# Order of ScalarE's work in a linear-attention and expert kernel: squares of q before den's logarithm, statistics split, exponentials in pairs

## The chip, the cores and the metric

The kernel runs on one NeuronCore of a Trainium2 chip, as one program. The metric is the time of one execution on the device in microseconds; the median of three runs counts, and one more execution was taken with the hardware profiler. In the rows below PE is TensorE, PEld its weight loads, DVE is VectorE, ACT is ScalarE, POOL is GpSimd and SP is SyncE, whose queue (SPq) issues most of the transfers.

## The reference, cut to what matters

x has 16 batches of 512 tokens of width 128. The layer is an adaptive layer norm block: attention with random features, then a feed-forward part in which each token goes to one of eight experts.

```python
mod = (silu(c) @ wmod).reshape(16, 6, 1, 128)      # sa, ca, ga, sb, cb, gb; ga and gb kept away from 0
h = layernorm(x) * (1 + ca) + sa
q, k = feature(h @ Wq.T + bq), feature(h @ Wk.T + bk)     # 16 heads of 8, 32 features each
#   feature(u) = (exp(u @ orf.T / 8**0.25 - sum(u*u) / (2 * sqrt(8))) + 1e-6) / sqrt(32)
kv, ksum = k^T v, sum_l k
attn = (q kv) / (q ksum)
x = x + ga * (attn @ Wo.T + bo)
h = layernorm(x) * (1 + cb) + sb
e = argmax(h @ gate_W + gate_b)
x = x + gb * (gelu(h @ W1[e] + b1[e]) @ W2[e] + b2[e])
```

All of it is computed in fp32.

## The kernel before, in words

Each engine has a program of its own, written out by hand; the order on an engine is the order in the code, and semaphores tie the engines together. There is no planner. The first stage runs `over_batches`: for each of the 16 batches every engine's `batch(b, ...)` runs once. Work on three neighbouring batches is interleaved: the features and attention of batch b, the projections of b+1, the residual and second norm of b-1, the gate and ranks of b-2.

PE's order in a batch (L1261 to L1294) is: `k_features` (L1145, L1148), `transpose_h2` (L1222), `v_project` (L1130), `out_project` of b-1 (L1214), `gate` (L1229), `q_features` (L1165), the gate transpose, `transpose_xn` of b+1 (L1115), `kv_product` (L1181), `project` k of b+1 (L1123), `rank`, `kv_transpose` (L1190), `project` q of b+1, `attend` (L1198, L1202 den, L1205 numerator).

ScalarE's order (L625 to L654): four exponentials of k (L609), v values, four exponentials of q (L615) with `modulate` of b+1 (L571, makes hT) in their middle, `kvm_copy` (L590), for b+1 `k_values` (L578), `k_squares` (L582) and `q_values` (L596), then Ln of den (L648), Exp of its negative (L650, a first value of 1/den in rden), `q_squares` of b+1 (L600), and half of the first norm of b+2 (L565).

VectorE's `attention` takes rden, refines it in two steps (L820, L823) and writes oT (L827), which `out_project` waits for. Ahead of it stand the masked kv (L806), the ranks, eps (L816) and the second norm's scaling of h2 (L725, L736); behind it, at the head of the next `batch`, `x_stats` (L702, four bn_stats, for b+3), the other half of the first norm (L774), the residual (L835) and its statistics (L842). The statistics feed GpSimd's `rstd1_of`, which raises to the power -0.5 (L466).

q's features need the values of q and their squares side by side in one row group. SP's `mix_q` copies them there: two transfers of qvals (L363), issued when q_values is done, then two of qsqs (L366) when q_squares is done, both into qmix, which `q_features` waits for. In the same queue stand the fetches of x, of the modulation rows and of the expert weights.

At the start, PE multiplies the modulation: columns for the first norm (L1103, L1104), then rows in two products (L1107 into bank KV, L1108 into bank G), and VectorE makes the modulation rows of them (L780 to L797); after that come the statistics of batch 1 and `normalise1` of batch 1 (L774).

The second stage has NBLK = 71 blocks of 128 tokens, each of one expert. For block k PE does `hidden` (L1319), the transpose of block k+1 (L1312) and `second` of k-2 (L1332); ScalarE Gelu (L682); VectorE three steps of `result` (L1044 to L1049); GpSimd the indirect store (L535). The block table for the first EARLY = 45 blocks is made before the last batches are routed, the rest later. SP fetches the blocks twelve ahead (`load_block`, L424), and among its fetches writes a padding row block behind each of the eight expert lists (L436); the blocks from 45 on are fetched only when the paddings have landed.

Of the kernel before, what the change touches and what calls it, by code (L numbers as in the profile page):

```python
# [21 lines left out]
F32 = mybir.dt.float32  # L22
# [10 lines left out]
P = 128  # L33
# [12 lines left out]
EARLY = (KNOWN * L - E * (P - 1) + P - 1) // P  # L46
PITCH = NT * P + P
# [32 lines left out]
R_END = R_NORMQ + P  # L80
# [33 lines left out]
def build(nc, x, weights, consts, rows, wmod, firsts, w2, out):  # L114
# [3 lines left out]
    with ExitStack() as ctx:  # L118
# [5 lines left out]

        def sem(name):
            return ctx.enter_context(nc.semaphore(name))
# [10 lines left out]
        feat_q = sb("feat_q", [P, 2, P // 2])  # L137
        bv_cols = sb("bv_cols", [P, D])
# [29 lines left out]
        kf = sb("kf", [P, LT, NC, 2, HP + 1])  # L168
# [41 lines left out]
        kf_row = kf[:, :, :, :, :].rearrange("p t c j k -> p (t c j k)")  # L210
# [3 lines left out]
        F = [pb("ps_feat0"), pb("ps_feat1")]  # L214
        KV, G = pb("ps_kv"), pb("ps_den")
        H, I = pb("ps_out"), pb("ps_gate")
        PJ = [pb("ps_proj0"), pb("ps_proj1")]
# [3 lines left out]
        QB = [F[0], F[1], PJ[0], PJ[1]]  # L221
        Q_ORDER = (2, 3, 0, 1)
        QB0 = [F[0], F[1], G, I]
        counts = [H[:, 0:E], I[:, 2 * P + LT * E:2 * P + LT * E + E]]
# [110 lines left out]
        def _(sp):  # L335
# [57 lines left out]
            mix_q(0)  # L393
# [35 lines left out]
            for k in range(EARLY - E):  # L429
                load_block(k)  # L430

            sp.wait_ge(s_cnti, 1)
            for e in range(E):
                load_block(EARLY - E + e)
                count = sp.value_load(cnt_i[0:1, e:e + 1], min_val=0, max_val=NT * P)
                sp.dma_start(lists[bass.ds(count + e * PITCH, P), :], padding[:]).then_inc(s_pad, 16)  # L436
            for v in range(B - HOMES, B):
                sp.wait_ge(s_scat[v % HOMES], scattered(v))
# [113 lines left out]
        def _(act):  # L552
# [54 lines left out]
            def k_feature(b, c):  # L607
                act.wait_ge(s_feat, 2 * NC * b.v + c + 1)
                a.activation(kf[:, :, c, :, 0:HP], QB[c][:, :].rearrange("p (t j m) -> p t j m", t=LT, j=2), ACT.Exp)\  # L609
                    .then_inc(s_exp, 1)  # L610

            def q_feature(b, n, first=False):
                act.wait_ge(s_feat, 2 * NC * b.v + NC + n + 1)
                c = Q_ORDER[n]
                a.activation(qf[:, c, :], (QB0 if first else QB)[c][:, :], ACT.Exp).then_inc(s_exp, 1)  # L615

# [8 lines left out]
            def batch(b, first=False, second=False, last=False, ahead=True):  # L625
                k_feature(b, 0)
                if not first and not second:
                    h2T_copy(b + -2)
                k_feature(b, 1)
                k_feature(b, 2)  # L630
                k_feature(b, 3)
# [3 lines left out]
                q_feature(b, 0, first)  # L635
                q_feature(b, 1, first)
                if not last:
                    modulate(b + 1)
                q_feature(b, 2, first)
                q_feature(b, 3, first)  # L640
                kvm_copy(b)
                if not last:
                    k_values(b + 1)
                    k_squares(b + 1)
                    q_values(b + 1)
                act.wait_ge(s_den, b.v + 1)
# [4 lines left out]
                if not last:  # L651
                    q_squares(b + 1)
# [43 lines left out]
        def _(dve):  # L696
            v = nc.vector

            def x_stats(b, slot):

                for t in range(LT):
# [58 lines left out]
            dve.wait_ge(s_modc, 1)  # L760

            v.tensor_copy(sa[:], F[0][:, 0:B])
            v.tensor_scalar(ca1[:], F[0][:, B:2 * B], 1.0, None, ALU.add).then_inc(s_cols, 1)

# [13 lines left out]
            normalise1(Batch(0), lo=LT // 2)  # L778
            dve.wait_ge(s_modp, 1)
# [193 lines left out]
            def batch(b, first=False, second=False, last=False, ahead=True):  # L973
# [4 lines left out]
                if ahead:  # L978
# [3 lines left out]
                    dve.wait_ge(s_x[(b + 3).par], 16 * (b + 3).half + 16)  # L982
                    if b.par == 0:
                        first_moments(b.half + 2, marked=x_stats(b + 3, 1))
                    else:
                        x_stats(b + 3, 0)
# [28 lines left out]
                if last:  # L1015
                    for k in range(1, R4 - 1):
                        copy_firsts(k)
                attention(b)
                if last:
# [13 lines left out]
                                   op0=ALU.mult, op1=ALU.add).then_inc(s_fq, 1)  # L1033
# [420 lines left out]
```

## Time and profile before

| | us |
|---|---|
| median of 3 runs | 364.83 (364.52 to 366.34) |
| the profiled execution | 363.67 |
| its span in the trace | 361.9 |
| PE busy in the span | 340.8 (94%) |
| DVE, ACT, POOL busy | 269.2, 270.1, 214.1 |

The page gives busy time by engine, a strip of 40 slices, the transfers, the chain of work that ended last, and the costliest groups of instructions. A timeline row gives the start, the length, the engine, the source line, the operation, what it writes and reads, how many instructions the row merges, and in brackets how long the engine had been idle before it and what released it. Matmuls are pipelined: a row's length reaches into the next row. An average over the span says little here, since the attention batches (to about 211 us) and the expert blocks have different limits; so the rows below are of single stretches.

### The profile page before, as it was taken

How to read it: one execution, taken by the hardware profiler on the slowest of the kernel's cores; microseconds unless marked ns; L12 is line 12 of the kernel's file. 1: busy time of each engine (PE TensorE's matmuls, PEld its weight loads, DVE VectorE, ACT ScalarE, POOL GpSimd, SP SyncE). 2: the span in 40 equal slices, each digit the busy share in tenths (PEclk: the TensorE clock that was granted, in tenths of full speed). 3: DMA queues.
4: the chain of work that ended last, by engine and by line, in shares of the span. 5: the costliest groups of instructions: out<-in, count | busy, mean ns of one | idle time of the engine just before them, and what ended most of it. 6: DMA issues, size and time to landing. Idle time of an engine off the chain costs nothing.

```text
span 361.9 us, 13820 instructions
## 1 busy us (share of the span) xinstructions
PE 340.8 (94%) x4835; PEld 265.8 (73%) x4835; DVE 269.2 (74%) x1103; ACT 270.1 (75%) x708; POOL 214.1 (59%) x262
## 2 busy tenths in 40 slices
PE   7799998899999999999999899999999998999993
PEld 6546664665566566646665679999999997999993
DVE  3706887988898889878887978787777764666653
ACT  2668997898899888988998766666666665666761
POOL 3223285785786767857864618855767554445554
PEclk9989999999999999999999999999999999999999
DMA  6275456866665656434442466544655664645400
GB/s 220 79 247 205 132 192 217 270 217 203 193 240 166 199 192 229 163 129 160 154 144 87 165 170 210 153 139 128 188 177 179 201 213 135 194 122 152 126 37 12
DMA packets 40532, 60.94 MB, mean 168 GB/s; under 512 B 5490, under 2 KB 28278, under 8 KB 40336
## 3 DMA queue, kind: packets, MB, share of 16 engines
q1 hardware_dynamic: 34096, 43.00, 39.6%
q0 software_dynamic: 6368, 17.05, 12.4%
q8 instruction: 41, 0.67, 0.8%
q14 instruction: 27, 0.22, 0.2%
HBM read 28.56 MB, written 19.34 MB: 132 GB/s over the span
## 4 chain that ended last, share of the span: by engine, by line
PE 51%; ACT 17%; DMA 12%; issue 6%; SPq 6%; DVE 3%; POOL 3%; DVEq 0%; POOLq 0%; ACTq 0%
PE ps_proj L1332 12%; DMA qmix<-qsqs 8%; PE ps_feat L1319 7%; PE ps_proj L1123 6%; ACT qf L615 4%; PE ps_proj L1165 4%; PE ps_den L1319 3%; PE ps_kv L1319 3%; ACT shared L571 3%; ACT shared L578 2%; ACT qvals L596 2%; POOL out L535 2%; ACT den L648 2%; PE ps_out L1312 2%; PE ps_kv L1214 2%
## 5 line engine op out<-in xcount | busy, mean ns | idle before, releaser
L535 POOL DMA_INDIRECT out<-kf,modb x71 | 70.5, 993 | 53.4 <-DVE kf L1049 46.5
L497 POOL DMA_INDIRECT experts_lists<-pay,slot x64 | 66.1, 1034 | 42.2 <-DVE slot L883 28.1
L1332 PE MATMUL ps_proj<-w2sb,qf 128*128 x568 | 74.8, 275 | 0.0
L1332 PEld LDWEIGHTS ps_proj<-w2sb,qf 128*128 128x128 f32 x568 | 68.9, 192 | 0.1
L673 ACT ACTIVATE xT<-ps_out 128x128 f32<-128x128 f32 x71 | 19.7, 277 | 46.2 <-PE ps_out L1312 46.1
L1044 DVE TENSOR_TENSOR kf<-ps_proj,firsts_sb 128x128 f32<-128x128 f32 x71 | 20.6, 290 | 36.9 <-PE ps_proj L1332 26.3
L682 ACT ACTIVATE qf<-ps_feat,shared 128x128 f32<-128x128 f32 x144 | 40.9, 374 | 0.0
L1319 PE MATMUL ps_feat<-xT,shared 128*128 128x128 f32 x288 | 38.7, 277 | 1.2 <-issue 0.7
L1319 PEld LDWEIGHTS ps_feat<-xT,shared 128*128 128x128 f32 x288 | 35.0, 192 | 2.4 <-issue 1.7
L1123 PE MATMUL ps_proj<-shared,wsb 128*128 128x512 f32 x62 | 33.3, 620 | 1.3 <-ACT shared L571 0.4
L967 DVE COPY shared<-firsts_sb 128x516 f32 x71 | 30.7, 433 | 1.3 <-issue 1.2
L1145 PEld LDWEIGHTS ps_feat<-feat_w,shared 32*128 32x128 f32 x256 | 19.4, 186 | 13.1 <-ACT shared L582 13.1
L1145 PE MATMUL ps_feat<-feat_w,shared 32*128 32x128 f32 x256 | 26.5, 283 | 0.5 <-ACT shared L582 0.5
L1145 PE MATMUL ps_proj<-feat_w,shared 32*128 32x128 f32 x256 | 26.5, 283 | 0.0
L1148 PE MATMUL ps_feat<-csb,shared 32*128 32x128 f32 x256 | 24.9, 270 | 0.0
L1148 PE MATMUL ps_proj<-csb,shared 32*128 32x128 f32 x256 | 24.9, 270 | 0.0
L615 ACT ACTIVATE qf<-ps_proj 128x512 f32<-128x512 f32 x30 | 16.3, 595 | 10.6 <-PE ps_feat L1165 10.6
L1047 DVE TENSOR_TENSOR kf<-kf,modb 128x128 f32<-128x128 f32 x71 | 21.3, 300 | 2.4
L1049 DVE TENSOR_TENSOR kf<-kf,modb 128x128 f32<-128x128 f32 x71 | 20.9, 294 | 2.4
L1165 PE MATMUL ps_proj<-qmix,feat_q 32*64 32x512 f32 x120 | 16.3, 611 | 5.7 <-DMA qmix<-qsqs 5.1
L491 POOL TENSOR_TENSOR xall<-xall,bog 128x512 f32<-128x512 f32 x16 | 20.5, 1281 | 1.3
L1312 PE MATMUL ps_out<-csb,modb 128*128 128x128 f32 x71 | 19.4, 274 | 1.8 <-DMA modb<-experts_lists 1.7
(189 smaller groups left out, 898.8 us busy)
## 6 DMA issues: line engine op xcount, KB each, us to landing
modb<-experts_lists SPq DMA_DIRECT2D x71, 196.0 KB, 2.6
xall<-in_x SPq DMA_DIRECT2D x16, 256.0 KB, 3.0
qmix<-qvals SPq DMA_DIRECT2D x32, 128.0 KB
qmix<-qsqs SPq DMA_DIRECT2D x32, 128.0 KB
pay<-modb SPq DMA_DIRECT2D x16, 256.0 KB, 2.8
modb<-modulation_rows SPq DMA_DIRECT2D x4, 768.0 KB, 5.1
firsts_sb<-in_firsts SPq DMA_DIRECT2D x8, 322.0 KB
w2sb<-in_w SPq DMA_DIRECT2D x8, 256.0 KB
```

Source lines behind the costliest of these rows:

```text
L497: g_.indirect_dma_start(out=lists, in_=pay[b.home][:, t, :], in_offset=None, out_offset=bass.IndirectOffsetOnAxis(ap=slot[b.home][:, t:t + ...
L535: g_.indirect_dma_start(out=rows_out, in_=yb[u], in_offset=None, out_offset=bass.IndirectOffsetOnAxis(ap=token, axis=0), bounds_check=last ...
L615: a.activation(qf[:, c, :], (QB0 if first else QB)[c][:, :], ACT.Exp).then_inc(s_exp, 1)
L682: ins = a.activation(g[k % R4][:, c * P:(c + 1) * P], HID[k % R4][:, c * P:(c + 1) * P], ACT.Gelu, bias=firsts_c[k % R4][:, WB1 + c:WB1 + ...
L967: v.tensor_copy(firsts_c[k % R4], firsts_sb[:, bass.ds(expert[k] * WB, WB2)]).then_inc(s_fc, 1)
L1123: mm((bank or PJ[i])[:, :], wsb[:, i * P:(i + 1) * P], hT[:], start=True, stop=True).then_inc(s_proj, 1)
L1145: mm(QB[c][:, tokens], kvals[at, tokens], feat_w[at, :], start=True, stop=False)
L1148: ins = mm(QB[c][:, tokens], ksqs[at, tokens], norm_w[at, :], start=False, stop=True)
L1165: ins = mm(bank[c][n * HP:(n + 1) * HP, :], feat_q[at, n, :], qmix[at, n, :], start=True, stop=True)
L1312: tr(XT[:, 0:P], xin[k % U][:, H2:H2 + D], ident).then_inc(s_bt, 1)
L1319: ins = mm(HID[u % R4][:, c * P:(c + 1) * P], firsts_c[u % R4][:, c * P:(c + 1) * P], xT[u % 2][:], start=True, stop=True)
L1332: ins = mm(Y[u % 2][:, 0:D], g[u % R4][:, c * P:(c + 1) * P], w2sb[:, bass.ds(e * DFF + c * D, D)], start=(c == 0), stop=(c == FC - 1))
```

## The change

In the batches, q_squares(b+1) moves on ScalarE ahead of Ln and Exp of den(b). VectorE takes the statistics of the first two tiles of batch b+4 ahead of `attention(b)`, and only those of the last two tiles at their old place. The eight exponentials of a batch become four, each over two neighbouring PSUM banks; for that the feature tile kf is laid out by channel first, and the banks are allocated in pairs. The waits on their count are rewritten.

At the start, batch 0 makes q's features without qmix: a second weight tile feat_v multiplies qvals and a third multiplies qsqs, into the same banks, and SP's `mix_q(0)` goes. The two products of the modulation rows stand behind the transposes of batch 0 and behind its two projections, in place of 12 fill-in matmuls; the copies of the modulation columns stand behind the half of the first norm.

In the block stage the paddings are written beside the fetches of blocks 33 to 40 in place of 37 to 44, and in the last turn `second(68)` stands ahead of `hidden(70)`.

```diff
+PADS_FROM = EARLY - E - 4
...
-            mix_q(0)
...
-            for k in range(EARLY - E):
+            for k in range(PADS_FROM):
                 load_block(k)
             sp.wait_ge(s_cnti, 1)
             for e in range(E):
-                load_block(EARLY - E + e)
+                load_block(PADS_FROM + e)
                 count = sp.value_load(cnt_i[0:1, e:e + 1], min_val=0, max_val=NT * P)
                 sp.dma_start(lists[bass.ds(count + e * PITCH, P), :], padding[:]).then_inc(s_pad, 16)
+            for k in range(PADS_FROM + E, EARLY):
+                load_block(k)
...
+            def k_pair(b, n):
+
+                act.wait_ge(s_feat, 2 * NC * b.v + 2 * n + 2)
+                a.activation(kf[:, 2 * n:2 * n + 2, :, :, :].rearrange("p c t j k -> p (c t j) k")[:, :, 0:HP],
+                             QP[n][:, :, :].rearrange("p c (g m) -> p (c g) m", m=HP), ACT.Exp).then_inc(s_exp, 1)
+
+            def q_pair(b, n, first=False):
+
+                act.wait_ge(s_feat, 2 * NC * b.v + NC + 2 * n + 2)
+                c = Q_ORDER[2 * n]
+                a.activation(qf[:, c:c + 2, :], (QP0 if first else QP)[c // 2][:, :, :], ACT.Exp).then_inc(s_exp, 1)
...
                     q_values(b + 1)
+                    q_squares(b + 1)
                 act.wait_ge(s_den, b.v + 1)
                 act.wait_ge(s_eps, b.v + 1)
                 a.activation(den[:], G[:], ACT.Ln, bias=kveps[:, 1:2]).then_inc(s_denp, 1)
                 act.wait_ge(s_denp, b.v + 1)
                 a.activation(rden[:], den[:], ACT.Exp, scale=-1.0).then_inc(s_rden, 1)
-                if not last:
-                    q_squares(b + 1)
...
             normalise1(Batch(0), lo=LT // 2)
+            mod_columns()
             dve.wait_ge(s_modp, 1)
...
+                    tiles = range(LT) if first else range(LT // 2, LT)
                     if b.par == 0:
-                        first_moments(b.half + 2, marked=x_stats(b + 3, 1))
+                        first_moments(b.half + 2, marked=x_stats(b + 3, 1, tiles))
                     else:
-                        x_stats(b + 3, 0)
+                        x_stats(b + 3, 0, tiles)
...
+                if b.v + 4 < B:
+                    dve.wait_ge(s_x[(b + 4).par], 16 * (b + 4).half + 16)
+                    x_stats(b + 4, b.par, range(LT // 2))
                 attention(b)
...
+            v.tensor_scalar(feat_v[:], rsb[:, R_ORFQ:R_ORFQ + P], float(DH ** -0.25), None, ALU.mult).then_inc(s_fq, 1)
...
-            mm(KV[0:B, 0:3 * D], sc, wmod_sb[:, 0:3 * D], start=True, stop=True)
-            mm(G[0:B, 0:3 * D], sc, wmod_sb[:, 3 * D:6 * D], start=True, stop=True).then_inc(s_modp, 1)
...
+                if first:
+                    for c in Q_ORDER:
+                        at = slice(c * CW, (c + 1) * CW)
+                        mm(QB0[c][:, :], feat_v[at, :], qvals[at, :], start=True, stop=False)
+                    for c in Q_ORDER:
+                        at = slice(c * CW, (c + 1) * CW)
+                        mm(QB0[c][:, :], rsb[at, R_NORMV:R_NORMV + P], qsqs[at, :], start=False, stop=True).then_inc(s_feat, 1)
+                    return
...
             transpose_xn(start)
-            keep_busy(12)
+            mm(KV[0:B, 0:3 * D], sc, wmod_sb[:, 0:3 * D], start=True, stop=True)
             project(start, 0, first=True)
             project(start, 1, first=True, bank=I)
+            mm(G[0:B, 0:3 * D], sc, wmod_sb[:, 3 * D:6 * D], start=True, stop=True).then_inc(s_modp, 1)
...
+                if k == NBLK - 1:
+                    second(k - 2, e)
                 hidden(k)
```

## Rows read from the trace of the kernel before

**Rows 1.** The page's first line, the whole span.
```profile
span 361.9 us, 13820 instructions
```
**Rows 2.** Busy time by windows of one batch each: PE, PEld, DVE, ACT, POOL, clock, DMA.
```profile
47.60:60.60 13.00, 11.85 (x221) 7.43 (x220) 10.53 (x44) 10.90 (x22) 9.73 (x12) 1.00 0.63 210
85.79:97.80 12.01, 11.85 (x220) 7.43 (x220) 10.92 (x53) 10.90 (x22) 8.01 (x11) 1.00 0.65 207
```
**Rows 3.** Timeline of ScalarE in batch 6 and at the head of the next.
```profile
99.57 0.69 ACT L596 ACTIVATE qvals<-ps_proj,wsb 128x512 f32<-128x512 f32 x1
100.14 0.69 ACT L648 ACTIVATE den<-ps_den,kveps 128x512 f32<-128x512 f32 x1
100.86 0.63 ACT L650 ACTIVATE rden<-den 128x512 f32<-128x512 f32 x1
101.40 0.61 ACT L600 ACTIVATE qsqs<-qvals 128x512 f32<-128x512 f32 x1
...
106.61 1.09 ACT L615 ACTIVATE qf<-ps_proj 128x512 f32<-128x512 f32 x2 [0.41 <-PE ps_feat L1165]
```
**Rows 4.** Timeline of VectorE in the same batch.
```profile
100.19 1.14 DVE L736 SCALAR_TENSOR_TENSOR pay<-pay,rstd,modb 128x128 f32<-128x128 f32 x4
101.53 0.76 DVE L820 SCALAR_TENSOR_TENSOR ps_den<-ps_den,kveps,rden 128x512 f32<-128x512 f32 x1 [0.20 <-ACT rden L650]
...
103.05 0.75 DVE L827 SCALAR_TENSOR_TENSOR oT<-ps_kv,kveps,rden 128x512 f32<-128x512 f32 x1
```
**Rows 5.** Timeline of PE in the same batch.
```profile
97.47 0.31 PE L1190 MATMUL ps_den<-csb,kvT 128*128 128x128 f32 x1
...
103.94 1.07 PE L1214 MATMUL ps_kv<-wo,oT 128*128 128x128 f32 x8
...
107.23 1.11 PE L1181 MATMUL ps_kv<-kf,v 128*32 128x65 f32 x64
...
109.51 0.31 PE L1190 MATMUL ps_den<-csb,kvT 128*128 128x128 f32 x1
```
**Rows 6.** Timeline of SP's queue in the same batch, the copies into qmix.
```profile
100.28 1.12 SPq L363 DMA_DIRECT2D qmix<-qvals  x2
102.04 1.11 SPq L366 DMA_DIRECT2D qmix<-qsqs  x2
```
**Rows 7.** Timeline of PE: the output projections of batches 0, 1 and 14.
```profile
30.42 1.16 PE L1214 MATMUL ps_kv<-wo,oT 128*128 128x128 f32 x8
...
35.40 0.27 PE L1190 MATMUL ps_den<-csb,kvT 128*128 128x128 f32 x1
...
41.83 1.07 PE L1214 MATMUL ps_kv<-wo,oT 128*128 128x128 f32 x8
...
202.06 1.06 PE L1214 MATMUL ps_kv<-wo,oT 128*128 128x128 f32 x8
```
**Rows 8.** Timeline at the start, and one window with its clock (columns of rows 2).
```profile
9.13 0.66 PE L1115 MATMUL ps_out<-csb,shared 128*128 128x128 f32 x4
9.24 0.28 DVE L780 COPY modrow<-ps_den 16x128 f32<-16x128 f32 x1 [0.81 <-PE ps_den L1108]
...
14.85 1.12 DVE L774 TENSOR_SCALAR shared<-xall,rstd,shift 128x128 f32<-128x128 f32 x4 [1.83 <-POOL shift L468]
...
18.88 0.65 PE L1165 MATMUL ps_den<-qmix,feat_q 32*64 32x512 f32 x2 [2.52 <-DMA qmix<-qsqs]
...
21.39 1.80 PE L1181 MATMUL ps_kv<-kf,v 128*32 128x65 f32 x64
...
19.00:21.00 2.00, 2.00 (x19) 0.78 (x20) 0.00 (x0) 0.64 (x2) 0.00 (x0) 0.62 0.94 356
```
**Rows 9.** Timeline of PE around the first block of the late table.
```profile
303.60 0.33 PE L1312 MATMUL ps_out<-csb,modb 128*128 128x128 f32 x1 [1.73 <-DMA modb<-experts_lists]
303.80 1.15 PE L1332 MATMUL ps_proj<-w2sb,qf 128*128 x8
```
**Rows 10.** Timeline of GpSimd, the last store.
```profile
358.30 0.97 POOL L535 DMA_INDIRECT out<-kf,modb  x1 [0.30 <-issue]
```

## What the change will do: the prediction

> **What bounds the kernel now.** The program has two stages: sixteen batches of attention (to about 211 us of a span of 361.9 us [rows 1]) and then 71 expert blocks. I read the trace in three steps: busy time by windows, to see which engine fills a batch; then the timelines of the four engines over one batch, laid side by side; then the two ends of the program by themselves.
>
> Two windows of one batch each [rows 2] hold the same work. The one from 85.79 us lasts 12.01 us with PE busy 11.85; the one from 47.60 us lasts 13.00 with the same 11.85. So a batch costs 12.0 us when PE is full, and up to 1 us more when it isn't. From the output projection of batch 1 (41.83) to that of batch 14 (202.06) [rows 7] there are 13 periods in 160.23 us, a mean of 12.325: 4.2 us above 13 x 12.0. The chain of waits puts that excess on the landing of q's squares in qmix, for which L1165 waits.
>
> The reader should not stop there, since a second chain runs beside PE. In batch 6: the kv transpose L1190 starts at 97.47 [rows 5]; behind it ScalarE goes without a pause through kvm, k, q values (99.57), Ln of den (100.14), its Exp (100.86) and q's squares (101.40) [rows 3]; VectorE's reciprocal step L820 starts at 101.53, having waited for rden, and oT (L827) ends at 103.05 + 0.75 = 103.80 [rows 4]; the output projection L1214 starts at 103.94 [rows 5]. An idle PE would start it 0.04 behind oT (other rows of such a hand-over: Exp ends 101.49, L820 starts 101.53), so this chain has 0.14 - 0.04 = 0.1 us to give and no more. I measured L1190's start to oT's end at 6.33 here.
>
> **The change, part by part.** *q's squares ahead of Ln.* q_squares waits for q_values' end: 99.57 + 0.69 + 0.03 = 100.29. It is 0.61 long, and instructions in a row overlap by about 0.1 (99.57 + 0.69 = 100.26, yet Ln starts at 100.14), so it adds 0.52 and Ln starts at 100.81 in place of 100.14 [rows 3]: 0.67 later, and Exp, the three VectorE steps and oT with it. What it gives: SP issues the two qvals transfers from 100.28 for 1.12 us, so the first of qsqs cannot be issued at 100.91, when the data is there, but at 101.42, against 102.04 before [rows 6]: only 0.62 earlier. L1165 then asks 0.6 later and the data lands 0.62 earlier, 1.2 in all, which is more than the longest excess of a batch (1.0 [rows 2]). So every wait for qmix goes, and what is late next is oT. New cycle, from L1190's start: 6.33 + 0.67 + 0.04 = 7.04 to L1214's start; 5.57 from there to the next L1190 at 109.51 [rows 5], of which 0.05 was the wait for qmix, so 5.52; and 0.09 because L1214 now starts from an idle PE (1.16 long at 30.42, 1.07 at 103.94 [rows 7, 5]). Sum 12.65 a batch; over 13 periods 164.45 against 160.23: **+4.2 us**. Bounds: if the 0.1 of give is 0.2, 12.55 and +2.9; if a transfer is still late now and then, 12.75 and +5.5. I take 12.65, since batch after batch L1214 starts 0.12 to 0.14 behind oT as here.
>
> *Half of the statistics ahead of the reciprocal.* It moves two of four bn_stats (0.86 for four, so 0.43) in front of L820. VectorE's h2 scaling ends at 101.33 [rows 4], so the two end near 101.8, and rden now comes at 102.16: hidden, with 0.3 to spare (0.1 to 0.25 where GpSimd stretches L736 to 1.45). Behind oT the residual comes 0.4 earlier, but it was already waiting for L1214: nothing. Its new wait is for an x that was fetched over a batch before. Queued behind that wait are the reciprocal and all that hangs on it. Cost 0, bounds 0 and +0.3 a batch.
>
> *Paired exponentials.* Two single ones take 1.09, and ScalarE was idle 0.41 before them, waiting for PE [rows 3]. All four row groups of L1165 end together, so waiting for two banks costs nothing, and saving 0.07 to 0.2 a pair shortens idle time. Behind the first pair modulation meets the end of L1181 within 0.05, so PE gains nothing either. Cost 0, bounds -0.1 and +0.1 a batch. The Trainium skill (ScalarE: Activation LUTs, "What ACT_TABLE_LOAD costs") has back-to-back ACTIVATEs overlap by about 93 ns of a fixed 186; by an estimate from it a pair would save 0.09, inside the bounds above.
>
> *First chain.* q_features(0) loses its transfer: PE waited 2.52 us for it until 18.88 [rows 8]. What is late next is another: the transposes of batch 1 need normalise1(1), which stood at 14.85. The row products of the modulation (end about 9.2) are moved: the G half behind both projections. hT comes 0.9 earlier (the transposes, at 9.13 [rows 8], stood behind L1107 and L1108, while their input was there at 8.3), the projections, a ScalarE step later, run from 9.8 to 11.8, the G product to 12.5. VectorE's block that began at 9.24 now begins at 12.5, 3.25 later, and normalise1(1), which follows statistics and GpSimd's power step in a fixed row, moves from 14.85 to 18.1 and ends at 19.2; the transposes run from 19.3 in place of 20.3. feat_v adds 0.2 on VectorE and is ready at 16.5, q's features end near 17.9. Then L1181, 1.80 at the low clock (granted 0.62 in the window from 19 us, [rows 8]) and 1.11 at the full one [rows 5]. With the clock low as before the shift of L1190 is -1.1, at the full clock -2.1; I take the middle, -1.6. The extra 0.67 on the way to oT leaves -0.9 for L1214(0), at 29.5 in place of 30.42 [rows 7]. The period after it: 4.98 to L1190(1) (30.42 to 35.40 [rows 7]), 7.04 to L1214: 41.5 in place of 41.83: **-0.3 us**. Bounds -1.0 (full clock, no cold start) and +0.7 (nothing gained).
>
> *Padding.* SP's loop of eight loads and paddings starts four blocks earlier. Before, the load behind the last padding came late: PE stood 1.73 us until 303.60, and with the refill (the first products from an idle PE take 0.33 and 1.15) it cost 2.0 to 2.25 [rows 9]. The loads 33 to 36 that are pushed back wait for stores anyway, and each has 10 us until its use; the load in question moves about 9 us forward. **-2.2 us**, bounds -2.3 and -1.7.
>
> *Last results.* second(68) runs ahead of hidden(70). GpSimd's last stores follow each other at its own pace, 0.97 and 0.30 between, the last at 358.30 [rows 10]. Now result 68 is ready 0.9 earlier (eight products: L1214's 1.07 [rows 5] less the overlap), but hidden(70) and its Gelu come 0.9 later and the last product waits for that: store 70 at about 357.8. **-0.5 us**, bounds 0 and -0.8.
>
> **Sum.** Between batch 14 and block 0 VectorE's table work hangs on oT and shifts as it does. 363.67 (the profiled execution) + 4.2 - 0.3 - 2.2 - 0.5 = 364.9, so +1.2 us. The profiled execution lies 1.16 below the median of the three runs, 364.83; on the median that is **366.0**.
>
> **Rivals.** (1) *The chain through den has more give than I read.* Matmul ends in a trace are modelled; if oT may come 0.67 later without holding PE, only the waits for qmix go and the batch falls to 12.0: 13 x 12.0 = 156 in place of 160.2, with the start about 1 us better: 364.83 - 4.2 - 1.0 - 2.7 = 356.9. For it: PE was the full engine and its waits were for the DMA. Against: 0.1 us of give in all batches. Chance 0.10. The Trainium skill (DMA: Bandwidth & Descriptors, "Rules for kernel authors") says to issue a DMA early and wait on it late; by that rule alone this rival is the forecast. Half-way, at 12.35 a batch (PE regains some of it in hand-overs that I took as fixed), gives 366.0 - 3.9 = 362.1. Chance 0.12. (2) *The statistics hold the reciprocal up.* It decides where L736 ends later than rden minus 0.43, about 101.75 in the batch shown. Half of the batches have GpSimd beside L736; with 0.2 to 0.4 more in each of 14, +2.8 to +5.6: 368.8 to 371.6. Against: L736 ends at 101.33 and the new rden has moved away from it. Chance 0.10. (3) *The start gives nothing*, since the modulation rows moved behind the projections hold statistics, power step and batch 1: +1.0, 367.0. Chance 0.15. (4) *A transfer still late*, for the four transfers now meet w2's and firsts' loads in another order: 12.75 a batch, 367.3. Chance 0.08.
>
> **How the numbers follow.** The forecast itself has 0.45, with 364.8 to 367.2 as its own range. All cases within 0.8 of the range's middle bounds give 362.0 to 368.6, which leaves out the full form of rival 1 and most of rival 2. Half a per cent, about what a measurement here can tell from no change, is 1.8 us: 363.0 to 366.65. Faster: rival 1 with its half-way form, 0.22, and little else: 0.23. Slower: rivals 2 to 4 (0.33, of which 3 a good part) and the upper third of the forecast (0.12), less what of rival 3 stays inside: 0.35. Within: 0.42.
>
> **What would show each step.** Right: L1190's start to L1214's start 7.0 in place of 6.47; the batches even, 12.6 to 12.7, with PE idle 0.5 before L1214 and no wait of L1165 for qmix; L820 still released by rden; PE's stall at 303 gone; last store 0.5 behind its place. Wrong: L1214 still back to back with L1130 (rival 1); L820 directly behind bn_stats (rival 2); a batch-1 transpose not before 20.3 (rival 3); L1165 released by qmix (rival 4).

## The result, and the profile after

Twenty runs of the changed kernel have a median of 366.72 us (364.07 to 369.39), against 363.69 us (360.17 to 369.43) for twenty of the kernel before on the same chip: a ratio of 1.0107, with a 95% interval from 1.0084 to 1.013. The change makes the kernel about 1.1% slower. The prediction said 366.0 us, 1.2 above before; the absolute time was met more closely than the difference, which is 3.0 us between the medians.

The profiled execution took 369.39 us, the longest of its twenty. This matters below: split at a mean granted clock of TensorE of 0.995, the runs of the changed kernel have medians of 365.8 (clock above) and 368.4 us (below), and those of the kernel before (29 runs beside the second set of experiments) 362.0 and 365.1. The two profiles are therefore compared by stage.

The span and two windows, each from one output projection to the next (columns as in [rows 2]):

```profile
span 367.6 us, 13729 instructions
...
57.00:69.51 12.51, 11.62 (x218) 7.04 (x216) 9.75 (x41) 9.95 (x19) 7.82 (x10) 1.00 0.76 243
69.51:82.74 13.23, 12.06 (x219) 7.56 (x219) 10.83 (x52) 10.49 (x19) 9.81 (x14) 1.00 0.65 218
```

Before, a good batch took 12.01 us with PE busy for nearly all of it [rows 2]; now the best take 12.51, and others still take 13.2 to 13.4. ScalarE in one batch, answering to [rows 3]:

```profile
103.22 0.69 ACT L606 ACTIVATE qvals<-ps_proj,wsb 128x512 f32<-128x512 f32 x1
103.94 0.63 ACT L610 ACTIVATE qsqs<-qvals 128x512 f32<-128x512 f32 x1
104.48 0.67 ACT L657 ACTIVATE den<-ps_den_gate,kveps 128x512 f32<-128x512 f32 x1
105.18 0.63 ACT L659 ACTIVATE rden<-den 128x512 f32<-128x512 f32 x1
...
111.03 1.03 ACT L627 ACTIVATE qf<-ps_proj 128x1024 f32<-128x1024 f32 x1 [0.52 <-PE ps_feat L1186]
```

VectorE (answers to [rows 4]), PE ([rows 5]) and SP's queue ([rows 6]) in the same batch:

```profile
104.90 0.48 DVE L709 BATCH_NORM_STATS2 st<-xall 128x6 f32<-128x128 f32 x2
105.84 0.76 DVE L829 SCALAR_TENSOR_TENSOR ps_den_gate<-ps_den_gate,kveps,rden 128x512 f32<-128x512 f32 x1 [0.46 <-ACT rden L659]
...
107.36 0.75 DVE L836 SCALAR_TENSOR_TENSOR oT<-ps_kv,kveps,rden 128x512 f32<-128x512 f32 x1
```

```profile
108.17 1.16 PE L1235 MATMUL ps_kv<-wo,oT 128*128 128x128 f32 x8 [0.42 <-DVE oT L836]
109.26 0.42 PE L1250 MATMUL ps_den_gate<-h2T,wsb 128*32 128x128 f32 x8
109.86 0.66 PE L1186 MATMUL ps_proj<-qmix,feat_q 32*64 32x512 f32 x4 [0.18 <-DMA qmix<-qsqs]
...
113.87 0.31 PE L1211 MATMUL ps_den_gate<-csb,kvT 128*128 128x128 f32 x1
```

```profile
103.94 1.11 SPq L372 DMA_DIRECT2D qmix<-qvals  x2
105.09 2.16 SPq L375 DMA_DIRECT2D qmix<-qsqs  x2
```

Ln starts 1.26 behind q_values where it started 0.57 behind it. VectorE now has 0.46 idle before the reciprocal, and PE 0.42 idle before the output projection, which ran without a pause before. Yet two rows on, L1186 still waits for the squares' landing. PE's waits over the whole span (what waited, for what: us in total, times, longest) show that both are general:

```profile
PE ps_kv L1235 <- DVE oT L836: 6.4, 15, 0.8
PE ps_proj L1186 <- DMA qmix<-qsqs: 2.7, 6, 0.8
```

The output projections of batches 0, 1 and 14, answering to [rows 7]:

```profile
32.01 1.16 PE L1235 MATMUL ps_kv<-wo,oT 128*128 128x128 f32 x8 [0.80 <-DVE oT L836]
...
44.01 1.16 PE L1235 MATMUL ps_kv<-wo,oT 128*128 128x128 f32 x8 [0.42 <-DVE oT L836]
...
209.76 1.16 PE L1235 MATMUL ps_kv<-wo,oT 128*128 128x128 f32 x8 [0.30 <-DVE oT L836]
```

The start, answering to [rows 8], first the G half of the row products and what hangs on it, then two windows:

```profile
14.54 0.90 PE L1325 MATMUL ps_den_gate<-qf,silu 128*16 128x384 f32 x2
...
15.47 0.28 DVE L789 COPY modrow<-ps_den_gate 16x128 f32<-16x128 f32 x1 [7.42 <-PE ps_den_gate L1325]
...
21.17 1.12 DVE L782 TENSOR_SCALAR shared<-xall,rstd,shift 128x128 f32<-128x128 f32 x4 [1.78 <-POOL shift L478]
```

```profile
9.00:13.00 4.00, 4.00 (x8) 1.38 (x7) 0.00 (x0) 0.84 (x2) 0.00 (x0) 0.50 0.13 52
13.00:16.00 3.00, 3.00 (x24) 0.80 (x27) 0.53 (x3) 2.52 (x4) 0.00 (x0) 0.71 0.00 0
```

The granted clock is 0.50, the lower of its two levels (1.2 GHz), from 9 to 13 us. The place of the old stall [rows 9], one block's steps without a pause, and the last store ([rows 10]):

```profile
302.25 0.27 PE L1334 MATMUL ps_out<-csb,modb 128*128 128x128 f32 x1
302.36 1.06 PE L1354 MATMUL ps_proj<-w2sb,qf 128*128 x8
303.25 1.06 PE L1341 MATMUL ps_feat<-xT,shared 128*128 128x128 f32 x8
...
361.50 1.15 PE L1354 MATMUL ps_proj<-w2sb,qf 128*128 x8 [0.43 <-ACT qf L689]
...
364.02 0.97 POOL L545 DMA_INDIRECT out<-kf,modb  x1 [0.60 <-DVE kf L1064]
```

Summed by stage, after less before: to the output projection of batch 1, 44.01 - 41.83 = +2.2 us (predicted -0.3); its next 13 periods, 165.76 - 160.23 = +5.5 (predicted +4.2); from batch 14 to the first block, -0.2; from there to the last store, -1.8 (predicted -2.7). Together +5.7, the difference of the spans.

### The profile page after: what moved, and what is told of

The parts are those of the page before. It is cut to its first block, busy times and chain, and to the rows that moved or that the text cites. A ratio compares the mean times of both kernels' runs of the same rounds, so it can differ in the third digit from the quotient of the medians.

```text
span 367.6 us, 13729 instructions
## 1 busy us (share of the span) xinstructions
PE 345.1 (94%) x4823; PEld 265.6 (72%) x4823; DVE 269.2 (73%) x1104; ACT 266.9 (73%) x644; POOL 213.5 (58%) x262
## 4 chain that ended last, share of the span: by engine, by line
PE 53%; ACT 18%; DVE 10%; DMA 7%; issue 4%; SPq 3%; POOL 1%; DVEq 1%; POOLq 0%; ACTq 0%
PE ps_proj L1354 16%; PE ps_feat L1341 9%; DMA qmix<-qsqs 6%; PE ps_proj L1136 5%; PE ps_den_gate L1341 4%; PE ps_proj L1186 4%; PE ps_kv L1341 4%; ACT shared L588 3%; ACT qf L627 3%; PE ps_kv L1235 3%; ACT qvals L606 2%; ACT shared L592 2%; ACT kvm L600 2%; PE ps_out L1334 2%; DVE ps_den_gate L829 2%
## 5 line engine op out<-in xcount | busy, mean ns | idle before, releaser
L1136 PE MATMUL ps_proj<-shared,wsb 128*128 128x512 f32 x62 | 34.3, 636 | 0.9 <-ACT shared L581 0.2
L1158 PEld LDWEIGHTS ps_feat<-feat_w,shared 32*128 32x128 f32 x256 | 19.6, 186 | 12.5 <-ACT shared L592 11.8
L1235 PE MATMUL ps_kv<-wo,oT 128*128 128x128 f32 x120 | 17.4, 288 | 6.4 <-DVE oT L836 6.4
L627 ACT ACTIVATE qf<-ps_proj 128x1024 f32<-128x1024 f32 x15 | 15.4, 1029 | 8.7 <-PE ps_feat L1186 8.7
L689 ACT ACTIVATE qf<-ps_den_gate,shared 128x128 f32<-128x128 f32 x72 | 20.5, 374 | 1.4 <-PE ps_den_gate L1341 1.4
```

Source lines behind the costliest of these rows:

```text
L627: a.activation(qf[:, c:c + 2, :], (QP0 if first else QP)[c // 2][:, :, :], ACT.Exp).then_inc(s_exp, 1)
L689: ins = a.activation(g[k % R4][:, c * P:(c + 1) * P], HID[k % R4][:, c * P:(c + 1) * P], ACT.Gelu, bias=firsts_c[k % R4][:, WB1 + c:WB1 + ...
L1136: mm((bank or PJ[i])[:, :], wsb[:, i * P:(i + 1) * P], hT[:], start=True, stop=True).then_inc(s_proj, 1)
L1158: mm(QB[c][:, tokens], kvals[at, tokens], feat_w[at, :], start=True, stop=False)
L1235: ins = mm(bank[:, t * P:(t + 1) * P], oT[:, t * P:(t + 1) * P], wo[:], start=True, stop=True)
```

## The experiments

Three theories had to be told apart. A: the squares' 0.67 us on the way to oT make the batch longer, whatever the transfers do. B: the landing in qmix still sets the batch. C: the statistics ahead of the reciprocal do. Beside them stood the questions what the start cost and what the two edits of the block stage gave. The first four kernels ran on a chip on which the kernel before took 385.05 us (29 runs); there PE also paused in places where the other chips show none, and the changed kernel itself was not run. Each ratio is against the kernel before on the same chip.

**Each part of the batch by itself.** The changed kernel with the squares put back:

```diff
                     q_values(b + 1)
-                    q_squares(b + 1)
...
                 a.activation(rden[:], den[:], ACT.Exp, scale=-1.0).then_inc(s_rden, 1)
+                if not last:
+                    q_squares(b + 1)
```

> The changed kernel with q's squares again behind Ln and Exp of den; all else as changed. The chain theory (den's chain, lengthened by the squares, sets the batch): from kv transpose to output projection falls from 7.04 back to about 6.4 us, the fastest batches from 12.50 to 12.0, and the mean of 13 batches from 12.75 to about 12.3, that is 5 to 6 us off the changed kernel: ratio to the kernel before about 0.995 to 0.998. Rival (the split statistics or the pairs set it): the batch stays at 12.5 and the ratio at 1.01.

384.22 us, ratio 0.9995 (0.9953 to 1.0038), a little above the 0.995 to 0.998 that was expected. The opposite, the squares alone moved ahead in the kernel before:

> The kernel before with nothing changed but q's squares put ahead of Ln. Chain theory: fastest batches 12.5 in place of 12.0, waits for qmix still there in some (mean 12.75), so 13 x 0.43 = 5.6 us more than before: ratio 1.012 to 1.016, more than the whole change. Rival (the start makes the loss, the batches only trade one wait for another): ratio 1.000 to 1.003.

388.48 us, ratio 1.0133 (1.0066 to 1.02). From the kv transpose to oT's end it shows 6.98 to 7.00 us in batches 2 to 14, as the changed kernel does (6.32 to 6.35 before), and its shortest period is 12.57. So the squares alone carry a loss as large as that of the whole change, and putting them back takes it away: theory A. The statistics put back to behind oT, with the squares left ahead:

```diff
-                    tiles = range(LT) if first else range(LT // 2, LT)
+                    tiles = range(LT)
...
-                if b.v + 4 < B:
-                    dve.wait_ge(s_x[(b + 4).par], 16 * (b + 4).half + 16)
-                    x_stats(b + 4, b.par, range(LT // 2))
                 attention(b)
```

> The changed kernel with all four statistics of x behind the attention steps, as before. Chain theory: the two that stood ahead of the reciprocal were hidden while VectorE waited for rden, and behind it the residual waits for PE: batch and ratio as in the changed kernel, 1.009 to 1.012. Rival (they hold the reciprocal up): batch falls by 0.2 to 0.4, ratio 1.000 to 1.004.

387.32 us, ratio 1.0073 (1.0036 to 1.0109), a little below the 1.009 to 1.012 expected and above the rival's 1.004, and again 6.98 to 7.00 us to oT's end. With the squares ahead, the statistics change nothing on this path: against theory C. But the run with the squares back shows 6.64 to 6.73 us in seven of 15 batches, and 6.43 to 6.47 in four, where the kernel before has 6.33, so C is true of another kernel than the changed one; a run further down settles that.

**The start.** The changed kernel with both row products and their 12 fill-in matmuls at their old place:

```diff
+            mm(KV[0:B, 0:3 * D], sc, wmod_sb[:, 0:3 * D], start=True, stop=True)
+            mm(G[0:B, 0:3 * D], sc, wmod_sb[:, 3 * D:6 * D], start=True, stop=True).then_inc(s_modp, 1)
...
             transpose_xn(start)
-            mm(KV[0:B, 0:3 * D], sc, wmod_sb[:, 0:3 * D], start=True, stop=True)
+            keep_busy(12)
             project(start, 0, first=True)
             project(start, 1, first=True, bank=I)
-            mm(G[0:B, 0:3 * D], sc, wmod_sb[:, 3 * D:6 * D], start=True, stop=True).then_inc(s_modp, 1)
```

> The changed kernel with the two products of the modulation rows again ahead of the transposes of batch 0 and the 12 fill-in matmuls back; q's features of batch 0 still made without qmix. Theory (the move took PE's cover at the start, so its clock was granted at half and the rows came 6 us late): granted clock about 1.0 from 9 to 13 us, the rows' first copy near 9.3 in place of 15.5, output projection of batch 0 near 29 in place of 32.0, and 2 to 3 us off: ratio about 1.003. Rival (the profiled run's start was an accident of one run): ratio stays 1.010 within 0.002.

384.58 us, ratio 1.0003 (0.9964 to 1.0041). The clock is 1.00 throughout the start, the row copy stands at 9.01 us, and the first output projection at 28.01, 4.0 earlier than in the profile of the changed kernel. A changed start at the full clock has it at 28.84 (below), so by itself the move of the row products costs about 0.8 us, and the low clock the other 3.2. The three are single traces of different chips, in which the first norm starts at 7.46, 7.18 and 7.29 us, so the split is good to some 0.3 us only.

**The changed kernel once more**, beside the next kernels on a chip like the first (before: 363.88 us, 29 runs):

> The changed kernel itself, as the mark for the others on the same chip. The pair of chips so far differ (before at 364 and at 385 us). Chain theory: its batches run from kv transpose to output projection in 7.0 us at least wherever PE is not late itself, and the ratio is 1.007 to 1.013. Rival (its loss belongs to the first chip only): 1.000 to 1.003.

366.07 us, ratio 1.0047 (1.0012 to 1.0083). That is less than the 1.007 to 1.013 expected: the interval ends just below that of the first measurement (1.0084 to 1.013), and it does not go below 1. So the loss is there again, but its size is known only as 0.5 to 1.1%. In this trace too all batches from 2 on have 7.04 or 7.05 to the output projection.

**Squares back and rows first together.**

> The changed kernel with both suspects undone: squares behind Ln and Exp, the products of the modulation rows and the 12 fill-in matmuls ahead of batch 0's projections. If the two losses are what the theory says and add up, it keeps the gains (batch 0 without qmix, padding, last results) without them: ratio 0.985 to 0.992. Rival (they overlap, or the gains are none): 0.995 to 1.000.

361.23 us, ratio 0.9938 (0.9909 to 0.9967): faster than both kernels, but short of the 0.985 to 0.992 expected. What is left of theory C shows in its rows. ScalarE's rden, then VectorE:

```profile
86.64 0.63 ACT L658 ACTIVATE rden<-den 128x512 f32<-128x512 f32 x1
```

```profile
87.30 0.47 DVE L710 BATCH_NORM_STATS2 st<-xall 128x6 f32<-128x128 f32 x2
87.70 0.74 DVE L830 SCALAR_TENSOR_TENSOR ps_den_gate<-ps_den_gate,kveps,rden 128x512 f32<-128x512 f32 x1
```

rden is there at 87.27, but the two statistics start only at 87.30, and the reciprocal follows them with no wait of its own, 0.43 behind rden. To oT's end it is 6.70 here (from 83.25 to 89.95). Seven of 15 batches are like it (6.64 to 6.72), in four it is 6.42 to 6.49, and in four 6.29 to 6.34 as before.

**The two edits of the block stage alone**, in the kernel before:

```diff
-            for k in range(EARLY - E):
+            for k in range(PADS_FROM):
...
+                if k == NBLK - 1:
+                    second(k - 2, e)
```

> The kernel before with the padding's new place and the new order of the last block alone. By the prediction's terms -2.2 and -0.5 us, that is a ratio of 0.992 to 0.994, with PE's stop at the first late block (1.73 us in the kernel before) gone and the last store earlier by 0.5. Rival (SP reaches the late blocks only when it has to, the stop only moves): 0.998 to 1.001.

362.86 us, ratio 0.9982 (0.9941 to 1.0023): not to be told from no change by the ratio, where 0.992 to 0.994 was expected. In its trace the time from the first block to the last store is 145.77 us where before it is 146.86, so they give 1.1 us; in the changed kernel 1.8. Its clock was 1.00 at 19 to 22 us, where that of before was 0.58, and its first output projection stood at 28.58 in place of 30.42, though nothing in that stretch differs: the start of the kernel before varies by itself.

**The copies of the values left out.** From batch 2 on the qvals copies are not made, so q's features there use old values (this part of the computation is wrong, and only its time is read):

```diff
-                for n in range(2):
-                    sp.dma_start(qmix[n::2, n, :], qvals[n::2, :]).then_inc(s_qmix, 16)
+                if v == 1:
+                    for n in range(2):
+                        sp.dma_start(qmix[n::2, n, :], qvals[n::2, :]).then_inc(s_qmix, 16)
...
-                pe.wait_ge(s_qmix, 64 * b.v)
+                pe.wait_ge(s_qmix, 32 * b.v + 32)
```

> The changed kernel without the copies of q's values into qmix from batch 2 on (the values of batch 1 stay there, so q's features are those of wrong values: that part of the computation is left out). Theory (the copies of the squares, though issued earlier, stand in SP's queue behind those of the values and land no sooner): the second issue of the squares takes 0.6 us in place of 1.4 to 2.1, no batch waits for qmix, and 13 batches take 13 x 12.5 = 162.5 us. Rival (other traffic, x and weights and scatters, holds the landing): issue and waits as in the changed kernel, 165 to 166 us.

363.38 us in its one run. Every period of the 13 is 12.50 to 12.52, 162.60 us in all, and no wait for qmix is left:

```profile
115.87 1.16 PE L1236 MATMUL ps_kv<-wo,oT 128*128 128x128 f32 x8 [0.41 <-DVE oT L837]
117.32 0.66 PE L1187 MATMUL ps_proj<-qmix,feat_q 32*64 32x512 f32 x4
```

So 12.5 us is what den's chain costs by itself, and the 3.2 us above it in the changed kernel (165.76 - 162.60) come with the copies of the values. Leaving them out does two things at once: it takes two transfers away, and it lets SP issue the squares' copies 0.45 us earlier still (3.51 us behind the kv transpose in place of 3.96), since the values' copies hold SP's queue for 1.11. This run also began at a granted clock of 1.00 and had its first output projection at 28.84.

**Other traffic.** Two kernels move what else stands in SP's queue. In the changed kernel, all loads of the expert weights moved behind the batches:

```diff
-                if 2 <= v < 2 + E:
-                    load_firsts(v - 2)
...
-                if 5 <= v < 5 + E:
-                    load_w2(v - 5)
...
+            for e in range(E):
+                load_firsts(e)
+                load_w2(e)
```

> The changed kernel with the loads of the expert weights (w2 and the first layer's) moved behind the batches; one look, since the blocks may start later for it. If these loads hold back the landing in qmix, the waits for qmix (3.3 us over 13 periods) go and every period is 12.5: 13 periods 162.6-163.2 us, as without the copies of the values. If not, the 13 periods stay at 165-166.5 us.

The 13 periods take 165.99 us, with waits of 3.0 us for qmix: nothing gained in the batches (384.38 us in all, one run, since the blocks then wait for their weights).

**The squares, the row products and the statistics put back**; kept are the direct features of batch 0, the pairs, the padding and the last results. This kernel and the three around it (weights late, gate rows, fill-ins) ran on a third chip, on which the kernel before took 364.57 us (29 runs):

> The changed kernel with q's squares behind Ln and Exp, the row products with their 12 fill-ins and the statistics all at their old places; kept are the direct q features of batch 0, the pairs, the padding and the last results. If the statistics held the reciprocal up once the squares are back (6.73 us from the kv transpose to oT's end in place of 6.33), this falls to 6.33 again, the fastest period of a batch to 12.0, the 13 periods to 159.5-161.5 us, and the ratio to the kernel before is 0.988-0.992. If the 0.4 us was something else (the pairs' new layout, say), the chain stays at 6.7, the 13 periods near 163, and the ratio is near 0.994.

359.67 us, ratio 0.9881 (0.9847 to 0.9914), the fastest of all. To oT's end it is 6.29 to 6.35 again in 14 of 15 batches and 6.40 in one, so the 0.4 was the statistics. Its shortest periods are 11.86, below the 12.00 of the kernel before. But the 13 together take 160.99, since the waits for qmix have grown to 6.8 us:

```profile
100.08 1.08 PE L1234 MATMUL ps_kv<-wo,oT 128*128 128x128 f32 x8
...
102.44 0.66 PE L1185 MATMUL ps_proj<-qmix,feat_q 32*64 32x512 f32 x4 [0.92 <-DMA qmix<-qsqs]
```

```profile
PE ps_proj L1185 <- DMA qmix<-qsqs: 6.8, 9, 1.3
```

In that kernel, the gate rows of a batch (the second large transfer that SP issues in it) moved one turn of its loop, behind the next squares' copies:

```diff
-                    gate_rows(v)
+                if v - 1 >= HOMES:
+                    gate_rows_of(v - 1)
```

> The same kernel, and besides the gate rows of a batch, the other large transfer in SP's queue, are issued one turn of its loop later, behind the next copies of the squares. If that traffic is what holds back the landing in qmix, its waits shrink and the 13 periods fall towards 13 x 12.0 = 156 us (157-159), ratio 0.980-0.986. If the squares' copies land late by themselves (behind the values' copies in the same queue), nothing changes: the 13 periods within 0.7 us of the run with the gate rows in their place.

360.03 us, ratio 0.9905 (0.987 to 0.9939); 13 periods in 161.80, 0.8 more than without this move, and waits for qmix of 7.5 us. The gate rows now leave 7.6 us ahead of the next copies of the values in place of 3.4, and nothing is gained. Neither this traffic nor the weights hold the landing back. Not moved were the load of x that SP issues directly behind the squares' copies and GpSimd's scatters; either may still have a share in it.

**Fill-ins ahead of the first transposes.** The changed kernel with PE kept busy where it stood idle for 1.60 us before 8.42:

```diff
             start, end = Batch(0), Batch(B)
+            keep_busy(24)
             pe.wait_ge(s_xns, 1)
             transpose_xn(start)
```

> The changed kernel with 24 fill-in matmuls ahead of the transposes of batch 0, where PE was idle. If the granted clock of 0.50 at 9-13 us comes from the idle PE ahead of it, it is 0.9-1.0 here, the G row product ends near 12.5 in place of 14.5, the first output projection starts at 28.5-29.5 in place of 32.0, and the ratio to the kernel before is 0.995-1.002. If the low clock comes by chance, or from what PE did earlier, it stays at 0.5-0.7 and the first output projection at 30-32 us; the ratio stays 1.004-1.011.

```profile
9.00:13.00 4.00, 3.82 (x32) 1.52 (x34) 0.62 (x4) 2.75 (x5) 0.00 (x0) 1.00 0.14 49
```

The clock is 1.00 where it was 0.50, the G product starts at 11.52 in place of 14.54, and the first output projection at 28.90: as the theory said. The mean clock is 0.995 or more in 11 of its 12 runs, in the changed kernel in 11 of 20. Yet the time is 367.0 us, ratio 1.0104 (1.0065 to 1.0143), and not 0.995 to 1.002: that part was missed. Against the 11 runs of the changed kernel at that clock (365.8) it is 1.2 slower. Of this 0.4 is in its trace (the period from batch 0 to 1 is 12.36 in place of 12.00), and 0.6 is the chip (the kernel before, at that clock, has 362.6 us here and 362.0 on the other). The changed kernel itself was not run on this chip, so what the fill-ins gain in the median stays open; shown is only that they keep the clock up.

## Why the prediction was right or wrong

**Den's chain: right, to 0.01 us.** From the kv transpose to the output projection the text had 7.04. All batches from 2 on show 7.04 or 7.05, and 15 of the 16 output projections wait for oT (the row of L1235 above). Rival 1, by which PE would not notice, gave 0.22 of the chance and is excluded by the run that moves the squares alone. The rule that was set beside it (the Trainium skill, DMA: Bandwidth & Descriptors, "Rules for kernel authors") is to issue a DMA early and wait on it late. By itself it forecasts this kernel wrongly: the issue came 0.6 us earlier, and what it was bought with cost 0.5 us a batch.

**The rest of the cycle: mis-sized.** From the output projection to the next kv transpose the text had 5.52 + 0.09 = 5.61; it is 5.47. The output projection is 1.16 long, as the text had it. The term that was mis-sized is the sum of the two: 5.52 was read where the output projection starts without a pause, and it holds time that PE loses behind the gate matmuls. There q_features starts 0.53 behind their start in the kernel before (92.93 to 93.46) and 0.36 in the changed one (96.75 to 97.11), both in batches without a wait for qmix. It is not the pairs that took this away here. The kernel before with the squares alone ahead has single exponentials, and where PE waited for oT it has 5.46 or 5.47 too, and 0.38 behind the gate matmuls:

```profile
95.06 1.16 PE L1213 MATMUL ps_kv<-wo,oT 128*128 128x128 f32 x8
96.14 0.43 PE L1228 MATMUL ps_gate<-h2T,wsb 128*32 128x128 f32 x8
96.52 0.66 PE L1164 MATMUL ps_proj<-qmix,feat_q 32*64 32x512 f32 x4
...
100.53 0.32 PE L1189 MATMUL ps_den<-csb,kvT 128*128 128x128 f32 x1
```

The two kernels with pairs on the same chip have 5.46 to 5.48 where PE waited for oT. So in the changed kernel the price of 0 for the pairs was right. Where PE does not wait for oT they do give something: 5.39 with pairs (the squares, the row products and the statistics put back) against 5.53 without (the kernel before), and shortest periods of 11.86 against 12.00, that is 0.14 us a batch. That the lost time is a wait for the exponentials of k, of which a pair is 1.02 long and two single ones 1.09, is likely, but no run shows it by itself.

**"Every wait for qmix goes": wrong.** This is the step that cost most inside the batches: 12.5 a batch would have given 162.6, and it was 165.76. The text had the squares' copies land 0.62 earlier because they are issued 0.6 earlier. They are issued earlier (3.96 us behind the kv transpose in place of 4.57), but they land no earlier: by the semaphore records of the traces, of which some are missing, the last of the four copies of a batch lands 8.3 us behind the kv transpose in the mean of the last 14 batches (8.55 in the second trace of the changed kernel), against 8.1 before. From the squares' issue to the landing it is 4.25 us in place of 3.55. PE shows the same: where L1186 waits, it starts 8.7 to 9.4 us behind the kv transpose, and L1165 before 8.2 to 9.1. The issue of the pair takes 1.23 us at best in place of 1.10, and up to 2.79 in place of 2.18. Without the values' copies, which stand directly ahead of them in the same queue, the landing is at 7.2 in the mean and the waits vanish; with the weights or the gate rows out of the way they don't. So the landing hangs on the copies of the values and not on when the last two copies are issued alone. Whether that is their order in the queue or their sharing of the DMA engines was not separated. The text's margin was also thinner than it said: it set 1.2 us against a longest excess of 1.0, read from one window, while the trace has a period of 13.13 and a wait of 1.20 (at 69.45). The sum came near by luck: 12.65 was to be a cycle without waits, and the 12.75 measured is 12.5 and 0.25 of waits. Rival 4 (12.75 a batch, chance 0.08) had the size right, but put it down to the weights' loads, which the run with the weights late refutes.

**The statistics: right for the changed kernel, and for the reason given.** rden moved away from them, and VectorE idles 0.46 before the reciprocal. The other half was not said: they are hidden only by the squares' delay. With the squares back they cost 0.3 to 0.4 us in about half of the batches and 0.1 in a quarter, so the two parts of the change can't be judged one by one.

**The start: wrong in sign.** Predicted -0.9 for the first output projection, measured +1.6. Two steps failed. First, the projections were put at the full clock, from 9.8 to 11.8; they ran at 0.50 from 10.8 to 14.6, since PE, with the row products gone from in front of the transposes, was idle 1.60 us before 8.42. Everything that hangs on the G product moved with it: the row copy to 15.47 (predicted 12.5), the norm of batch 1 to 21.17 (18.1), its transposes to 22.35 (19.3). The direct features then take 2.0 us of PE's time where two rounds from qmix take 1.1. Second, the gain was counted from the 30.42 of one profile of the kernel before, which had a low clock of its own at 19 to 22 us. For the full clock the text's terms put the first output projection at 29.0 (30.42 - 2.1 + 0.67), and in the run without the copies of the values, at the full clock, it is at 28.84. But the kernel before at its full clock has it at 28.58: the third rival, the start gives nothing. That is the better statement of what this part is worth; 1.6 compares one profile at the low clock with another whose clock was low in another place.

**Padding: right in mechanism, smaller in size.** The stall of 1.73 us at 303 us is gone. From the first block to second(67), before's 139.13 us (212.41 to 351.54) are 137.44 after: -1.7, the smaller bound of the text, and -1.0 in the kernel with these edits alone. Part of it came back at the ranks of the late table, where PE waits 0.3 and 0.5 us for VectorE in the two kernels, and before shows no such wait.

**Last results: right in the danger, wrong in the sum.** From second(67) to the last store it is 6.68 us in place of 6.76, so 0.1 and not 0.5, at the bound of 0. The last product waits 0.43 for its Gelu, and the last store then waits for VectorE; its 0.30 pace, from which the text reckoned, no longer sets it (0.60 before the last store).

**In all.** With both kernels at the full clock the parts sum to +0.3 (start), +0.6 (batch 0 to 1), +5.5, -0.2 and -1.8: +4.4; the medians of the two groups at that clock differ by 3.8 (365.8 against 362.0). The text's +1.2 was too low by the start, the batches (12.75 in place of 12.65) and the block stage; that 366.0 lay so near 366.72 is due to the three runs of the kernel before that it started from, whose median was 1.1 above that of twenty.

## What to carry to other kernels

Before moving an instruction forward on an engine, read the slack of the chain that it is put in front of, at the hand-over: 0.14 us between oT's end and the output projection was the whole of it, and 0.67 put in front of it cost 0.5 in every batch, while the transfer that it was to hurry landed no earlier. An earlier issue did nothing for a transfer whose predecessors stand directly ahead in the same queue; leave the predecessors out once and see whether the wait goes. Take a change of several parts apart: here the direct first batch, the pairs and the padding give 1.2% (0.9881), which the squares, the statistics and the moved row products had turned into a loss of about 1%.

## What the runs showed of the hardware that was not expected

The granted clock of the start differs between traces of one and the same start: from 9 to 13 us it was 0.50 in two profiles of the changed kernel, 0.60 to 0.70 in three kernels with the same start, and 1.00 in a fourth. PE had been busy for 1.33 to 1.61 us from 6 to 9 us in the five where it fell, and for 2.46 in the one where it didn't. The kernel before has its low stretch later, at 19 to 22 us (0.58, but 1.00 in another run), behind the 2.52 us in which PE waited for qmix. Of 29 runs of it 21 had a mean clock under 0.995 and took 3.2 us more; of the 12 of the fastest kernel, with direct features and the rows first, none had. So a third of its 1.2% is that this low stretch does not occur: against the 10 runs of the kernel before beside it that had the full clock (362.6 us) its 359.67 is 2.9 us less, 0.8%.

The issue of the two copies of the squares takes 1.10 to 1.25 us at best and often more (up to 2.18 in the kernel before and 2.79 in the changed one), and SP's next issue stands behind it. And one chip of those used runs all these kernels 5.8% slower (385.05 against 363.88), with pauses of PE inside the features of k and in the blocks that no semaphore explains; the ratios on it still told the squares from the rest.
